# Edge layer of a four-layer GNN: message sums over 32 nodes in four column tiles, and the activations of two layers alternated

## What is computed

```python
# dst is sorted: dst = int(625 * u ** 2), u uniform in 0..1, then argsort
edge_feat = concat([x[src], x[dst], edge_attr], axis=-1)     # 20000 x (512 + 512 + 64)
h = mish(edge_feat @ W1 + b1)                                # 20000 x 512, layer one
messages = mish(h @ W2 + b2)                                 # 20000 x 512, layer two
agg = segment_sum(messages, dst, num_segments=625)           # sums over the edges of a target
u = mish(concat([x, agg], axis=-1) @ W3 + b3)
out = u @ W4 + b4                                            # then residual and layer norm
```

## Time and profile before

| | us |
|---|---|
| median of 3 runs (lowest, highest) | 1639.71 (1639.4, 1640.55) |
| the profiled execution | 1639.68, its span 1638.0 |
| busy PE, PEld, DVE, ACT, POOL | 1549.4, 1226.5, 1193.1, 1097.3, 672.7 |
| chain that ended last | PE 40%, DVE 3%, ACT 2% of the span |

### The profile page before, as it was taken

The page is one execution under the profiler, slowest core; times in us unless marked ns, Lnnn a source line. Parts: engine busy times, 40 slices in busy tenths (PEclk is TensorE's granted clock), DMA queues, the critical chain, the costliest instruction groups (busy, mean ns, idle before and its releaser), DMA issues. The chain is left out here.

```text
span 1638.0 us, 25185 instructions
## 1 busy us (share of the span) xinstructions
PE 1549.4 (95%) x8530; PEld 1226.5 (75%) x8530; DVE 1193.1 (73%) x1976; ACT 1097.3 (67%) x1534; POOL 672.7 (41%) x498
## 2 busy tenths in 40 slices
PE   5789899999999999999999999999999999999987
PEld 4765586878788878877854778787878787888774
DVE  8977646555565646465623499999999999999967
ACT  9841546544554546444530599999999999999963
POOL 3410200120012001200302788888888888888601
PEclk9999899999999999999999999999999999999989
DMA  3001320022012201212106767777777777777710
GB/s 106 0 20 66 92 83 26 15 68 87 26 33 84 77 1 33 81 36 78 41 1 222 160 142 148 146 150 150 148 152 148 152 150 148 149 149 150 170 39 32
DMA packets 107048, 153.95 MB, mean 94 GB/s; under 512 B 42043, under 2 KB 47035, under 8 KB 106467
## 3 DMA queue, kind: packets, MB, share of 16 engines
q0 software_dynamic: 72832, 87.84, 28.4%
q1 hardware_dynamic: 34146, 65.21, 12.6%
HBM read 141.02 MB, written 11.73 MB: 93 GB/s over the span
## 5 line engine op out<-in xcount | busy, mean ns | idle before, releaser
L1787 POOL DMA_INDIRECT edge_gathered<-dst_table,edge_index x158 | 262.0, 1658 | 58.7 <-issue 54.4
L223 PE MATMUL edge_z2p<-edge_w_hi,edge_h_hi 128*128 128x512 f32 x628 | 253.3, 403 | 2.6 <-DVE edge_late L2117 2.6
L223 PE MATMUL edge_z2p<-edge_w_lo,edge_h_hi 128*128 128x512 f32 x628 | 249.0, 396 | 0.0
L223 PE MATMUL edge_z2p<-edge_w_hi,edge_h_lo 128*128 128x512 f32 x628 | 248.8, 396 | 0.0
L1756 POOL DMA_INDIRECT edge_gathered<-src_table,edge_index x158 | 201.8, 1277 | 85.4 <-POOL edge_index L1750 30.6
L977 POOL TENSOR_TENSOR h<-h,tr_row_b 128x512 f32<-128x512 f32 x40 | 59.3, 1520 | 271.4 <-ACT C L1222 271.1
L966 POOL TENSOR_TENSOR tr_cw<-w_c,tr_cw 32x1024 fp32r<-32x1024 f32 x7 | 16.6, 2375 | 348.7 <-ACT tr_cw L1182 348.7
L223 PEld LDWEIGHTS edge_z2p<-edge_w_hi,edge_h_hi 128*128 128x128 f32 x628 | 118.4, 189 | 42.0 <-issue 16.9
L223 PEld LDWEIGHTS edge_z2p<-edge_w_hi,edge_h_lo 128*128 128x128 f32 x628 | 118.5, 189 | 28.5
L223 PEld LDWEIGHTS edge_z2p<-edge_w_lo,edge_h_hi 128*128 128x128 f32 x628 | 118.5, 189 | 25.0
L2134 DVE SCALAR_TENSOR_TENSOR edge_early<-edge_early,edge_z1p 128x1024 f32<-128x1024 f32 x79 | 96.4, 1220 | 48.9 <-ACT edge_early L2002 48.8
(11 more groups left out here) (366 smaller groups left out, 4020.0 us busy)
## 6 DMA issues: line engine op xcount, KB each, us to landing
w_c<-in_attr_T SPq DMA_DIRECT2D x78, 128.0 KB, 4.1
agg<-edge_sum_rows POOLq DMA_DIRECT2D x36, 128.0 KB, 10.7
w_a<-in_wv SPq DMA_DIRECT2D x4, 1024.0 KB, 5.3
w_b<-in_wq SPq DMA_DIRECT2D x4, 1024.0 KB, 5.4
w_a<-in_wk SPq DMA_DIRECT2D x4, 1024.0 KB, 7.7
w_b<-in_wo SPq DMA_DIRECT2D x4, 1024.0 KB, 6.8
w_a<-in_m SPq DMA_DIRECT2D x4, 1024.0 KB, 5.4
w_b<-in_m SPq DMA_DIRECT2D x4, 1024.0 KB, 5.5
```

The costliest lines, as they stand in the source:

```text
L223: mm = pe.matmul(out, a, b, start=(n == 0), stop=(n == last))
L1787: pool.indirect_dma_start(out=from_rows[ring][:, j, :].bitcast(F32), out_offset=None, in_=k.dst_table, in_offset=bass.IndirectOffsetOnAxis ...
```

## The change

Three things are changed.

1. The sums of the first 36 groups go over a window of 32 nodes (SUM_WIN) in place of 64. The 512 features are then cut into four parts (SIDES = 4) of 128, one for each of four column tiles of PE, where there were two parts of 256. The last four groups keep 64.
2. The edge layer has a table of window starts of its own, with no sharing between groups, and its own number of sweeps; the front makes the numbers for it.
3. ScalarE's and VectorE's orders within a step are changed: the activations of layer one and layer two alternate on ScalarE, and VectorE has the layer-two instruction ahead of the product of layer one.

```diff
                 own.wait()
                 step(dve.tensor_scalar(over[:, :], iota16[0:1, WIN:NP:WIN], span1[:, 0:1], None, ALU.is_le))
                 step(dve.tensor_reduce(span1[:, 1:2], over[:, :], AX.X, ALU.add))
-                dve.tensor_copy(k.starts[:, :], wtab[:, :]).then_inc(windows_known, 1)
-                dve.tensor_copy(k.sweeps[:, :], span1[:, 1:2]).then_inc(windows_known, 1)
+                dve.tensor_copy(starts[:, :], wtab[:, :]).then_inc(windows_known, 1)
+                dve.tensor_copy(k.sweeps[:, 0:1], span1[:, 1:2]).then_inc(windows_known, 1)
+                step(dve.tensor_copy(k.first_dst[:, :], ps_row[:, 0, :]))
+                step(dve.tensor_tensor(group_span[:, :], ps_row[:, 1, :], k.first_dst[:, :], ALU.subtract))
+
+                step(dve.tensor_scalar(group_span[:, GROUPS - LATE:], group_span[:, GROUPS - LATE:], float(WIN - SUM_WIN), None,
+                                       ALU.subtract))
+                step(dve.tensor_reduce(group_most[:, 0:1], group_span[:, :], AX.X, ALU.max))
+                step(dve.tensor_scalar(group_over[:, :], iota16[0:1, SUM_WIN:NP:SUM_WIN], group_most[:, 0:1], None, ALU.is_le))
+                step(dve.tensor_reduce(group_most[:, 1:2], group_over[:, :], AX.X, ALU.add))
+                own(dve.tensor_copy(k.sweeps[:, 1:2], group_most[:, 1:2]))
...
                 settle(k, pool)
                 for a in range(RING):
                     gather_src(a)
+                pool.wait_ge(S["last_ready"], 1)
                 pool.wait_ge(dst_stored, 16 * NT)
...
-                        pool.dma_start(k.agg[bass.ds(start, WIN), :].rearrange("n (s c) -> s n c", s=2),
+                        pool.dma_start(k.agg[bass.ds(start, SUM_WIN), :].rearrange("n (s c) -> s n c", s=SIDES),
                                        sum_rows[slot][:, :], accum_op=ALU.add).then_inc(sum_stored, 16)
...
                         for b in range(2):
                             for j in range(PT):
-                                for side in range(2):
-                                    mm = pe.matmul(ps_sum[slot][side * WIN:(side + 1) * WIN, 0:D // 2],
-                                                   onehot[slot][:, b * PT + j, :],
-                                                   h2[b][:, j * D + side * (D // 2):j * D + (side + 1) * (D // 2)],
+                                for side in range(SIDES):
+                                    mm = pe.matmul(ps_sum[slot][side * SUM_WIN:(side + 1) * SUM_WIN, 0:D // SIDES],
+                                                   onehot[slot][:, b * PT + j, 0:SUM_WIN],
+                                                   h2[b][:, j * D + side * (D // SIDES):j * D + (side + 1) * (D // SIDES)],
                                                    start=(b == 0 and j == 0), stop=(b == 1 and j == PT - 1))
                             mm.then_inc(S["pair_summed"], 1)
...
                     if on(2):
                         act.wait_ge(S["u1_ready"], s(-1))
                         act.activation(m1[one], m1[one], ACT.Square).then_inc(S["inner1_ready"], 1)
-                        act.wait_ge(S["inner1_ready"], s(-2) * 2 + 1)
-                        act.activation(m1[one], m1[one], ACT.Ln, bias=1.0).then_inc(S["inner1_ready"], 1)
-                        act.wait_ge(S["inner1_ready"], s(-1) * 2)
-                        act.activation(m1[one], m1[one], ACT.Exp, scale=-1.0).then_inc(S["q1_ready"], 1)
                     if on(4):
                         act.wait_ge(S["z2_ready"], s(-4) * PT + (PT if on(3) else 1))
                         if on(6):
 
                             act.wait_ge(S["h2_ready"], s(-5))
                         act.activation(m2[two], z2[two], ACT.Exp).then_inc(S["e2_ready"], 1)
+                    if on(2):
+                        act.wait_ge(S["inner1_ready"], s(-2) * 2 + 1)
+                        act.activation(m1[one], m1[one], ACT.Ln, bias=1.0).then_inc(S["inner1_ready"], 1)
                     if on(5):
                         act.wait_ge(S["log2_ready"], s(-4))
                         act.activation(m2[old], m2[old], ACT.Exp, scale=-1.0).then_inc(S["q2_ready"], 1)
+                    if on(2):
+                        act.wait_ge(S["inner1_ready"], s(-1) * 2)
+                        act.activation(m1[one], m1[one], ACT.Exp, scale=-1.0).then_inc(S["q1_ready"], 1)
...
                 dve.wait_ge(S["made"], 1)
                 own(dve.tensor_copy(iota[:, :], iota_i[:, :]))
+                own(dve.memset(wtab[:, :], 0.0))
+                own.wait()
+                spans = [1, SUM_SWEEPS, GROUPS]
+                own(dve.tensor_tensor(wtab[:, 0:SUM_SWEEPS * GROUPS].rearrange("p (w g) -> p w g", g=GROUPS),
+                                      iota[0:1, 0:NP:SUM_WIN][:, :, None].to_broadcast(spans),
+                                      k.first_dst[:, None, :].to_broadcast(spans), ALU.add))
+                own.wait()
+                dve.tensor_scalar(starts[:, :], wtab[:, :], float(NP), None, ALU.min).then_inc(S["last_ready"], 1)
...
-                            dve.tensor_scalar(sum_rows[slot][:, :], ps_sum[slot][:, 0:D // 2], -2.0, None, ALU.mult).then_inc(S["sum_taken"], 1)
+                            dve.tensor_scalar(sum_rows[slot][:, :], ps_sum[slot][:, 0:D // SIDES], -2.0, None, ALU.mult).then_inc(S["sum_taken"], 1)
+                    if on(4):
+                        dve.wait_ge(S["e2_ready"], s(-3))
+                        dve.tensor_scalar(m2[two], m2[two], TOP, 1.0, ALU.min, ALU.add).then_inc(S["u2_ready"], 1)
                     if on(2):
                         dve.wait_ge(S["q1_ready"], s(-1))
                         dve.scalar_tensor_tensor(m1[one], m1[one], 0.5, ps_z1[one][:, :], ALU.subtract, ALU.mult).then_inc(S["h1_ready"], 1)
-                    if on(4):
-                        dve.wait_ge(S["e2_ready"], s(-3))
-                        dve.tensor_scalar(m2[two], m2[two], TOP, 1.0, ALU.min, ALU.add).then_inc(S["u2_ready"], 1)
```

More of the change, by code:

```diff
@@ L42 @@
 MAXSWEEPS = NP // WIN
+SUM_WIN = 32
+SUM_SWEEPS = NP // SUM_WIN
+SIDES = P // SUM_WIN
+LATE = 4
 NORMED = 3
@@ L244, in front @@
         shared = sb("shared", [1, 2, SPANS])
-        wtab = sb("wtab", [1, (MAXSWEEPS + 1) * GROUPS])
+        starts = sb("starts", [1, (MAXSWEEPS + 1) * GROUPS], I32)
         span1, over = sb("span1", [1, 2]), sb("over", [1, MAXSWEEPS - 1])
+        group_span, group_most, group_over = sb("group_span", [1, GROUPS]), sb("group_most", [1, 2]), sb("group_over", [1, SUM_SWEEPS - 1])
         iota_i = sb("iota_i", [P, WIDE], I32)
@@ L592, in start_of @@
                 def start_of(u):
-                    return dve.value_load(k.starts[0:1, bass.ds(u, 1)], min_val=0, max_val=NP)
+                    return dve.value_load(starts[0:1, bass.ds(u, 1)], min_val=0, max_val=NP)
                 def compare_to(u, a, start):
@@ L1565, in edge_layer @@
     RING = 4
-    LATE = 4
     OWN = [(m, f) for m in range(KF) for f in range(2)]
@@ L1586, in edge_layer @@
         onehot = [sb(f"onehot{a}", [P, TPG, WIN]) for a in range(2)]
-        sum_rows = [sb(f"sum_rows{a}", [P, D // 2]) for a in range(2)]
+        sum_rows = [sb(f"sum_rows{a}", [P, D // SIDES]) for a in range(2)]
         own_part = sb("own_part", [P, KF, NP])
@@ L1594, in edge_layer @@
         last_dst = sb("last_dst", [P, TPG])
+        wtab, starts = sb("wtab", [1, (SUM_SWEEPS + 1) * GROUPS]), sb("starts", [1, (SUM_SWEEPS + 1) * GROUPS], I32)
         st, mv, rstd = sb("st", [P, NT, 6]), sb("mv", [P, NT, 2]), sb("rstd", [P, NT])
@@ L1652, in sweeps @@
         def sweeps(eng):
-            return eng.value_load(k.sweeps[0:1, 0:1], min_val=0, max_val=MAXSWEEPS - 1)
+            return eng.value_load(k.sweeps[0:1, 1:2], min_val=0, max_val=SUM_SWEEPS - 1)
         def run_steps(eng, step, between=None, begin=None):
@@ L1746, in copy_index @@
                     if last:
-                        pool.wait_ge(S["last_ready"], 2)
+                        pool.wait_ge(S["last_ready"], 3)
                     settle(k, pool)
@@ L1797, in step @@
                         slot = a // 2
-                        start = pool.value_load(k.starts[0:1, bass.ds(g(12), 1)], min_val=0, max_val=NP)
+                        start = pool.value_load(starts[0:1, bass.ds(g(12), 1)], min_val=0, max_val=NP)
                         pool.wait_ge(S["sum_taken"], g(10))
                         settle(k, pool)
-                        pool.dma_start(k.agg[bass.ds(start, WIN), :].rearrange("n (s c) -> s n c", s=2),
+                        pool.dma_start(k.agg[bass.ds(start, SUM_WIN), :].rearrange("n (s c) -> s n c", s=SIDES),
                                        sum_rows[slot][:, :], accum_op=ALU.add).then_inc(sum_stored, 16)
@@ L2098, in step @@
                     if a % 2 == 0 and on(6):
-                        start = dve.value_load(k.starts[0:1, bass.ds(g(6), 1)], min_val=0, max_val=NP)
-                        shape = [P, TPG, WIN]
```

(11 more changed lines are left out.)

6 lines of the change are left out of this document (4 added, 2 removed).

## The result

| | before | after |
|---|---|---|
| median of 4 runs (lowest, highest), us | 1639.76 (1639.4, 1640.55) | 1842.68 (1841.17, 1845.48) |
| the profiled execution, its span, us | 1639.68, 1638.0 | 1842.38, 1840.7 |
| busy PE, DVE, ACT, POOL, us | 1549.4, 1193.1, 1097.3, 672.7 | 1603.5, 1192.3, 1081.7, 665.5 |

The changed kernel takes 1.124 times as long (95% interval 1.1224 to 1.1257), 203 us more. It was forecast at 1835 us with a range of 1800 to 1885.

The account below looks back on a forecast made before the run. A DVE-ACT ring of 16.69 us per group was taken as the bound, PE 0.10 us behind. The terms: 1639.7 + 197.0 (new ring) - 3 (loop end) + 1.5 (front) = 1835 us, range 1800 to 1885.

Parts of the forecast that it names:

- The bound before: Edge layer loop: a DVE, ACT, DVE cycle through layer one takes 16.69 us per group; PE needs 16.59.
- The new ring: Edge layer loop: the new orders close a DVE-ACT cycle through both layers, 10.95 us per step, 76 steps, plus 197.0 us.
- two savings: In the new DVE-ACT cycle: narrower one-hot, at most 0.15 us; L2090 and a 1.33 us distance shortening, 0.22 + 0.08.
- The small terms: Outside the loop's cycle: -3 us at the loop's end, +1.5 in the front, 0 for the edge layer's tables.
- the -3: End of the loop: PE's work, before held back about a step, no longer is; -3 us, bounds 0 and -5.6.
- the front's seven instructions: Front, ahead of the first comparisons: seven one-partition instructions, each waited for, 0.22 us each, +1.5 us, bounds 0 and 2.
- The edge layer's tables: Start of the edge layer: three DVE instructions under DVE's 2.83 us wait for an attribute load, cost 0.
- The sums: PE's 1.88 us block per group: gain between nothing and 0.94 us, counting for nothing in the total time.
- What was to be seen: Loop signs: products 10.8 to 11.1 us apart, ACT waiting 3 us or more before L2020, PE about 70% busy.
- The rival of the clock: Loop: PE's clock falls and binds from a half-clock share of 0.57; 1884 us at 0.65; chance 0.08.
- The faster rival: Loop: DVE empties z2p before ACT reaches layer two's exp, ACT never stands, PE binds; 1603 us; chance 0.05.

Follow-up runs that it names:

- Loosening the ring alone: Kernel before, with DVE's attribute part moved from behind the split to just behind the first instruction of layer one: 1636.42 us, ratio 0.9996.
- Shortening PE's work alone: Changed kernel with both old orders of ACT and DVE put back, keeping the 32-node sums and new tables: 1635.94 us, ratio 0.9979.
- Both together: Changed kernel with both old orders, and the attribute part moved just behind the first instruction of layer one: 1615.78 us, ratio 0.9857.
- the attribute part in the wait: Changed kernel with DVE's attribute part moved from behind the split to just ahead of layer two's min and +1: 1797.65 us, one run.
- The kernel of 1615 us: Changed kernel with both old orders, and the attribute part moved just ahead of DVE's product of layer one: 1614.97 us, ratio 0.9857.

## Why the prediction was right

**The bound before: right.** The prediction had a ring of DVE and ACT as the bound, "with PE 0.10 us per group behind it". That is shown by the two halves. Loosening the ring alone stops at PE (steps of 7.94 and 8.63 us). Shortening PE's work alone stops at the ring (8.62 and 7.95). Both together get past either.

**The new ring: right, in place and in length.** The order alone, without a word of the sums changed, costs 204.9 us, and moving the attribute part out of the ring gives 45 back. The step with a one-hot, from start to start in the rows of the changed kernel above:

| from, to | predicted from the rows before, us | measured, us |
|---|---|---|
| product L2166 to split L2172 | 1.26 | 1.35 |
| L2172 to L2174 | 0.72 | 0.73 |
| to the attribute part L2112 | 1.14 | 1.14 |
| to L2118 | 0.39 | 0.34 |
| to L2125 | 0.59 | 0.61 |
| over the one-hot to L2146 | 1.47 | 1.33 |
| L2146 to ACT L2020 | 1.30 | 1.32 |
| L2020, L2023, L2026 to L2029 | 2.85 | 2.86 |
| L2029 to the product | 1.09 | 1.07 |
| sum | 10.81 | 10.75 |

The median from 1100 to 1500 us is 10.81. The other step is 11.26 (11.35). The prediction's mean step was 10.95, and it is 835.75 / 76 = 11.00. Of its two savings, the narrower one-hot came in full (1.33 for 1.47). In the step without a one-hot L2118 came (0.61 us to the next in place of 0.81), but L2125 to L2146 didn't (1.34). And 0.09 us went back in every step where the split waits for the product. Both losses set in with the fifteenth product: up to the fourteenth these two distances are 1.26 and 1.25 us, and the steps are 11.08 and about 10.66, which is the prediction's lower bound of 11.05 and 10.66.

**The small terms: two were off.** The sum was +197.0 us in the loop, -3 behind it, +1.5 ahead of it. Measured from the profiled executions, it is +200.5, -0.8 and +3.0, together 202.7. The loop and the part ahead of it are in these products of layer one, the first, third and last of the changed kernel:

```profile
919.21 1.22 DVE L2166 SCALAR_TENSOR_TENSOR edge_early<-edge_early,edge_z1p 128x1024 f32<-128x1024 f32 x1 [3.30 <-ACT edge_early L2029]
...
935.70 1.22 DVE L2166 SCALAR_TENSOR_TENSOR edge_early<-edge_early,edge_z1p 128x1024 f32<-128x1024 f32 x1 [1.35 <-ACT edge_early L2029]
...
1771.45 1.22 DVE L2166 SCALAR_TENSOR_TENSOR edge_early<-edge_early,edge_z1p 128x1024 f32<-128x1024 f32 x1 [2.14 <-ACT edge_early L2029]
```

The third stood at 932.68 and the last at 1567.92. From the last product to the end of the span it is 69.3 us after and 70.1 before, so of the -3 only -0.8 is there.

Ahead of the loop, the front's seven instructions cost 0.2 us where the edge layer begins on DVE, not 1.5. The edge layer's tables, which were put at 0 under DVE's wait of 2.83 us, are the step of the prediction that failed. That cover was DVE's own, and it held: DVE's wait for the load shrank to 0.70. But the change also makes POOL wait for the tables before its first gather by target (`pool.wait_ge(S["last_ready"], 1)` in the diff; the first instruction that raises this semaphore is L2094, the last of the tables). Nothing covers that. DVE and POOL of the changed kernel:

```profile
901.21 0.58 DVE L2094 TENSOR_SCALAR edge_starts<-edge_wtab 1x840 int32<-1x840 f32 x1
...
902.98 0.13 DVE L2106 CAST edge_last_dst<-edge_last_raw 32x1 f32<-32x1 int32 x1
```

```profile
903.31 1.59 POOL L1803 DMA_INDIRECT edge_gathered<-dst_table,edge_index  x1 [8.27 <-DVE edge_last_dst L2106]
```

The profile puts the wait down to L2106, the last on DVE that it saw before the gather, but the program doesn't wait for that one. L2094 ends at 901.79, and the gather begins 1.52 us later. Before, the last store to dst_table had landed at 900.68, and the gather began 1.51 us later, at 902.19. So 1.1 us are lost here, 0.2 of them the front's.

The first product is 2.0 us later than before, the third 3.0. The rest of the first 2.0 can be read from the trace as well. PE's first matmul on the gathered rows begins 8.33 us after that gather, where it was 8.05, so 0.3 are lost in the gathers. PE had stood idle for 2.74 us just before that matmul, where it was 1.55, and its clock is 0.71 from there on, where it was 1.00. Most of its matmuls with the attributes start 0.21 us apart in place of 0.12, so from the first matmul to ACT's first exp it is 2.53 us, where it was 1.94: 0.6 lost. PE's windows, the changed kernel and the one before:

```profile
908.00:911.60 3.60, 0.90 (x4) 0.31 (x2) 0.00 (x0) 0.53 (x1) 2.99 (x3) 1.00 0.87 159
911.60:914.20 2.60, 2.56 (x17) 2.56 (x18) 0.00 (x0) 0.03 (x1) 2.30 (x2) 0.71 0.98 154
```

```profile
910.20:912.20 2.00, 1.96 (x17) 1.94 (x18) 0.00 (x0) 0.02 (x1) 1.70 (x2) 1.00 0.88 142
```

The last 1.0 belongs to the step in which layer two begins, which is the first turn of the new ring.

**The sums: right.** PE's block went from 1.88 us to 1.01, from its start to the next product's. PE of the changed kernel:

```profile
1203.52 1.08 PE L1917 MATMUL edge_sump<-edge_late,edge_onehot 128*32 128x128 f32 x32 [0.81 <-DVE edge_late L2125]
1204.53 0.50 PE L227 MATMUL edge_z2p<-edge_w_hi,edge_h_hi 128*128 128x512 f32 x1
...
1214.93 0.49 PE L227 MATMUL edge_z2p<-edge_w_hi,edge_h_hi 128*128 128x512 f32 x1 [2.89 <-DVE edge_late L2146]
```

That is 0.87 of the upper bound of 0.94 us, so four column tiles of 32 get close to twice the rate of two tiles of 64. By this the trace agrees with the Trainium skill, "TensorEngine Tiling (Array Packing)", section Theoretical Speedup, which gives up to 4x for 32 columns where it gives up to 2x for 64. The prediction's "it counts for nothing here" holds too: the first row waits 0.81 us for DVE, and the third 2.89.

**What was to be seen.** The distances of two products (10.8 us, and 11.3, which is a little above the 10.8 to 11.1 that was said), the wait of about 1 us before L2163 and of 2 before L2166, and the chain over DVE and ACT came as said. Two points didn't. ACT's idle time is not "3 us or more" before L2020. It is split, 1.5 there and 1.5 to 2.0 before L2014, because ACT already stands waiting for L2118, which is in the ring as well. And PE is busy 81% and not 70%, which fits matmuls that run at half clock for part of the time.

**The rival of the clock: its condition came, its cost in the loop didn't.** The clock falls again and again, and its mean from 1100 to 1200 us is 0.90. But 0.90 = 1 - f/2 means that f = 0.2 of the time is at half clock, far from the 0.57 from which it was to decide. The Trainium skill, "TensorE: Matmul & The Clock Gate", section Why this matters for your kernels, warns that idle gaps between bursts of matmuls bring the lower clock. The trace agrees: it is 0.50 after the stretch in which PE worked 1.57 of 3.40 us. In the loop this costs nothing, while ahead of it, where PE is on the path, it cost the 0.6 us above. That PE is off the path in the loop is shown twice: the order alone gives PE a longer block of sums and has the same 11.27 us step without a one-hot, and the experiment with the attribute part in the wait gained its full length, with nothing changed in PE's program.

**The faster rival** needed DVE to empty z2p before ACT comes to the exp. ACT waits 1.49 us for that in the turn shown, and 54.4 / 36 = 1.5 us on average. The kernel of 1615 us shows that its time, 1603, can be approached, but by the old order. ACT's sixteen activations of a group, 16.01 us, are what is left in its way.

## What to carry to other kernels

When in-order engines serve two interleaved chains, write down for each step which instruction waits for which, and go round. Any cycle that closes once per step is a lower bound of the step whatever the busy shares say, and its length is the sum of the start-to-start distances of everything queued in it, the work of the other chain too. Here the interleaving saved about 0.3 us in dependent starts (an estimate from the earlier trace rows) and made the step 2.6 us longer (11.00 against 8.36). And where two bounds lie within 1% of each other (16.59 and 16.69 us here), each alone can be improved with almost no effect (0.2% and nothing here, 1.4% together). Test them together. Where work is hidden under one engine's wait, ask who else waits for that work: here POOL did, by a line of the change itself.

## What the runs showed of the hardware that was not expected

- The granted clock falls in a loop in which PE is busy four fifths of the time: after a stretch with 1.57 of 3.40 us busy, PE was granted 0.50 (1.2 of 2.4 GHz) for the next 3.30 us, and it was back at 1.00 over the 17 us after that.
- A dependent instruction's distance is not fixed. From the product to the split that reads it, it is 1.26 us up to the fourteenth product and 1.35 from the fifteenth on, with the same 1.22 us of work, in all three kernels where the two are neighbours (the changed kernel, the order alone, the attribute part in DVE's wait). From the message product to the instructions that empty z2p it goes from 1.25 to 1.34 between the thirteenth and the fifteenth product in all nine kernels, before and after among them. The fifteenth product stands in the first step of the hardware loop in `run_steps`. The sixteen steps ahead of it are unrolled, with constants as the values waited for, and in the loop these are computed from its counter. That this is the cause was not isolated.
- Half the bytes in an accumulating DMA shorten the transfer, but not always its instruction on POOL. In the old order the instruction took 2.25 us in the mean of 36 with 128 KB and 1.80 with 64 KB (the sums alone). In the new order it took 2.06 with 128 KB (the order alone) and 2.09 with 64. The median from issue to landing fell in both, from 10.7 to 6.0 us and from 10.2 to 5.8.
